# A graph network on one core: the stored one-hot matrix and the attention sums in f32, and a second score split into a linear word and a relu

## The reference

```
e = leaky_relu(x_l[src] + x_r[dst], 0.2) @ att
alpha = softmax of e over the edges of a destination (and a self loop)
out = segment_sum(alpha * x_l[src], dst) + bias
```

## Time and profile before

| what | value |
|---|---|
| median of three executions | 4830.54 us |
| profiled execution, its own time | 4824.61 us |
| span of the profile | 4822.8 us |
| message stage, first to last scatter | 303.6 to 1389.3 us |
| first attention, first gather to first row of the next stage | 1885.2 to 3003.7 us |
| second attention, first gather to first row of the next stage | 3107.5 to 4463.2 us |
| busy share of the span: PE, DVE, ACT, POOL | 49%, 58%, 13%, 56% |

### The profile page before, as it was taken

One profiled execution on the slowest core, in us unless ns is written; L12 is line 12 of the kernel. 1 busy time (PEld: TensorE's weight loads), 2 busy tenths in 40 slices (PEclk: granted clock), 3 DMA queues, 4 the chain that ended last, 5 costly groups with the idle time before them and its releaser, 6 DMA issues. The chain is left out here.

```text
span 4822.8 us, 75928 instructions
## 1 busy us (share of the span) xinstructions
PE 2356.4 (49%) x18851; PEld 1736.9 (36%) x18904; DVE 2781.6 (58%) x5419; ACT 647.4 (13%) x1473; POOL 2686.7 (56%) x2730
## 2 busy tenths in 40 slices
PE   0133333333306624666666665355555555555798
PEld 0023333333305513454544454233333333333232
DVE  8641111111118865777777777577877887877201
ACT  0001111111105410111111111011111111111000
POOL 0037777777745522777777774176666666663000
PEclk9955555555555555566666656555555555555899
DMA  0133334343315523555555552143333333332744
GB/s 21 38 123 124 125 122 130 126 129 123 114 36 109 107 47 85 140 144 148 143 147 147 143 146 78 42 102 94 94 95 91 91 97 92 94 95 60 275 170 168
DMA packets 533005, 537.07 MB, mean 111 GB/s; under 512 B 213790, under 2 KB 370324, under 8 KB 532618
## 3 DMA queue, kind: packets, MB, share of 16 engines
q1 hardware_dynamic: 243738, 289.79, 20.1%
q0 software_dynamic: 81072, 115.39, 10.7%
q10 hardware_dynamic: 208000, 130.01, 8.8%
HBM read 376.99 MB, written 159.58 MB: 111 GB/s over the span
## 5 line engine op out<-in xcount | busy, mean ns | idle before, releaser
L1381 POOL DMA_INDIRECT rows<-nodes_xl,id_slot x832 | 868.3, 1044 | 577.8 <-issue 240.9
L638 POOL DMA_INDIRECT msg_by_src<-message,place_slot x832 | 832.6, 1001 | 343.5 <-issue 252.8
L1381 POOL DMA_INDIRECT rows<-nodes_kv,id_slot x832 | 822.6, 989 | 339.8 <-issue 242.0
L1697 PE MATMUL counts_p<-hot_blocks 128*128 128x128 bf16 x2080 | 541.1, 413 | 362.3 <-DVE running_counts L1569 319.8
L599 PE MATMUL picked<-X,hotT 128*128 x1664 | 374.5, 423 | 674.2 <-issue 390.3
L599 PEld LDWEIGHTS picked<-X,hotT 128*128 128x128 f32 x1664 | 360.6, 331 | 688.0 <-issue 688.0
L560 DVE TENSOR_TENSOR message<-picked,w_dst 128x512 f32<-128x512 f32 x104 | 71.9, 691 | 845.7 <-ACT message L612 838.0
L1738 PE MATMUL sums<-parts,hot 128*128 128x68 bf16 (+1 forms) x4992 | 325.2, 251 | 374.9 <-DVE parts L1558 374.9
L1697 PEld LDWEIGHTS counts_p<-hot_blocks 128*128 128x128 bf16 x2080 | 277.5, 148 | 545.0 <-DVE running_counts L1569 339.1
L1738 PEld LDWEIGHTS sums<-parts,hot 128*128 128x128 bf16 x4992 | 311.8, 168 | 424.1 <-issue 424.1
L1569 DVE SCALAR_TENSOR_TENSOR running_counts<-running_counts,same_block,counts_p 128x128 f32<-128x128 f32 x1040 | 359.8, 346 | 171.0 <-DVE running_counts L1569 31.3
(11 more groups left out here) (343 smaller groups left out, 3606.2 us busy)
## 6 DMA issues: line engine op xcount, KB each, us to landing
adjacency<-running_counts ACTq DMA_DIRECT2D x1040, 64.0 KB
loc_all<-loc_by_cell SPq DMA_DIRECT2D x104, 512.0 KB
hotT<-hotT_by_step SPq DMA_DIRECT2D x208, 256.0 KB, 3.1
hot<-hot_by_step SPq DMA_DIRECT2D x208, 256.0 KB, 3.1
blocks<-adjacency SPq DMA_DIRECT2D x40, 1280.0 KB, 11.4
hot_by_step<-hot ACTq DMA_DIRECT2D x104, 256.0 KB, 2.0
hotT_by_step<-hotT ACTq DMA_DIRECT2D x104, 256.0 KB, 2.2
rows<-msg_by_src SPq DMA_DIRECT2D x312, 68.0 KB
```

Source lines behind the costliest of these rows:

```text
L638: pool.indirect_dma_start(out=msg_dram, out_offset=bass.IndirectOffsetOnAxis(ap=ids[:, s, t:t + 1], axis=0), in_=rows[:, s, t, :], in_offs ...
L1381: pool.indirect_dma_start(out=rows[:, j, t, :], out_offset=None, in_=table, in_offset=bass.IndirectOffsetOnAxis(ap=ids[:, j, t:t + 1], axis=0)
L1697: ins = nc.tensor.matmul(counts_p[:, q - HALVES[half][0], :], hot_b[:, r, 1, :, t], hot_b[:, r, 0, :, t], start=g == 0, stop=g == 1)
```

## The change

Four things are done.

- `hot` is f32 instead of bf16, in DRAM too (512 KB a step instead of 256). Line 567 reads the f32 lane number (repeated over the tiles) and the f32 places (repeated over the lanes), with the lane innermost, so that a tile's weights are contiguous. The two bf16 copies that it read go.
- The three parts, their two roundings on ScalarE and two subtractions on VectorE are gone. The sums are one f32 product for each tile, from `mixed` directly.
- `mixed` and `hot` have four slots, one for each step of a window. hot is loaded by SyncE in pairs in the steps s = 2 and 3, each behind a wait for the sums of the same slot one window before. `weigh` waits for the same sums.
- The second score is 0.2 y + 0.8 relu(y), y = x_l + x_r. The sum over words of 0.2 att x_l is one word per row, computed before the stage and stored as the 66th word of the table; the relu and the product with 0.8 att are one instruction; the word is added to the sum in a small one. The linear word of the destination is left out, for it is the same for all edges of a softmax.

The diff, cut to its core:

```
-        hot_dram = dram("hot_by_step", [STEPS, P, TB * P], BF16)
+        hot_dram = dram("hot_by_step", [STEPS, P, TB * P])
...
-                    step(v.tensor_copy(loc_h[:].rearrange("p j t -> p (j t)"), loc[:]))
...
-                    nc.vector.tensor_copy(lane_h[:], lane[:].unsqueeze(2).to_broadcast([P, P, TB])).then_inc(cleared, 1)
...
                         nc.vector.tensor_tensor(
-                            hot[:, s, :, :], lane_h[:],
-                            loc_h[:, bass.ds(i * NS + s, 1), :].rearrange("p a t -> p (a t)").unsqueeze(1).to_broadcast([P, P, TB]),
+                            hot[:, s, :, :], lane[:].unsqueeze(1).to_broadcast([P, TB, P]),
+                            loc[:, bass.ds((i * NS + s) * TB, TB)].unsqueeze(2).to_broadcast([P, TB, P]),
                             ALU.is_equal).then_inc(hot2_made[s], 1)
...
-                mixed = sbuf("mixed", [P, 2, TB, cols], ctx=c)
-                left = sbuf("left", [P, 2, TB, cols], ctx=c)
-                parts = sbuf("parts3", [P, 2, 3, TB, cols], BF16, ctx=c)
-                hot = sbuf("hot", [P, 8, P, TB], BF16, ctx=c)
+                mixed = sbuf("mixed", [P, 4, TB, cols], ctx=c)
+                hot = sbuf("hot", [P, 4, TB, P], ctx=c)
...
+                        def hot_loads(w, pair):
+
+                            for q in pair:
+                                if not (isinstance(w, int) and w == 0):
+                                    sp.wait_ge(scattered, w * 4 + q - 3)
+                                sp.dma_start(hot[:, q, :, :].rearrange("p t e -> p (t e)"),
+                                             hot_dram[bass.ds(w * 4 + q, 1), :, :].rearrange("a p e -> p (a e)")).then_inc(hot_in[q], 16)
...
-                            if w is not None and s >= 2:
-                                pair = (2 * s - 4, 2 * s - 3)
-                                for q in pair:
-                                    act.wait_ge(weighed, (w * 4 + q) * KM + KM)
-                                    if not (isinstance(w, int) and w == 0 and q < 2):
-                                        act.wait_ge(scattered, w * 4 + (q - 1))
-                                    nc.scalar.copy(parts[:, q % 2, 0, :, :], mixed[:, q % 2, :, :]).then_inc(high_made, 1)
-                                for q in pair:
-                                    act.wait_ge(left_made, w * 4 + q + 1)
-                                    nc.scalar.copy(parts[:, q % 2, 1, :, :], left[:, q % 2, :, :]).then_inc(middle_made, 1)
...
-                            if not (isinstance(w, int) and w == 0 and q < 2):
-                                dve.wait_ge(scattered, J - 1)
+                            if not (isinstance(w, int) and w == 0):
+                                dve.wait_ge(scattered, J - 3)
...
-                                    split(w, 0)
-                                    split(w, 1)
-                                    lowest_part(w, 0)
-                                    lowest_part(w, 1)
...
-                            pe.wait_ge(low_made, J + 1)
+                            pe.wait_ge(weighed, (J + 1) * KM)
                             for b, n in enumerate(ns):
                                 for t in (2 * b, 2 * b + 1):
-                                    for m in range(3):
-                                        ins = nc.tensor.matmul(sums[:, bass.ds(n, cols)], hot[:, p * 4 + q, :, t], parts[:, q % 2, m, t, :],
-                                                               start=False, stop=False)
+                                    ins = nc.tensor.matmul(sums[:, bass.ds(n, cols)], hot[:, q, t, :], mixed[:, q, t, :],
+                                                           start=False, stop=False)
...
-                    step(v.memset(xl[:, :, D:], 1.0))
+                    step(v.memset(xl[:, :, D:D + 1], 1.0))
+                    step(v.tensor_scalar(att_r[:], att_s[:], 0.8, None, ALU.mult))
+                    step(v.tensor_tensor(sq[:], lr[:, :, 0:D], rowwise(att_s[:]), ALU.mult))
+                    step(v.tensor_reduce(a[:], sq[:], AX.X, ALU.add))
+                    step(v.tensor_scalar(xl[:, :, D + 1], a[:], 0.2, None, ALU.mult))
...
-                step(v.scalar_tensor_tensor(leaky[:], product[:], 0.2, product[:], ALU.mult, ALU.max))
-                step(v.tensor_tensor(product[:], leaky[:], att_s[:].unsqueeze(1).to_broadcast([P, TB, D]), ALU.mult))
+                step(v.scalar_tensor_tensor(product[:], product[:], 0.0, att_r[:].unsqueeze(1).to_broadcast([P, TB, D]),
+                                            ALU.max, ALU.mult))
                 step(v.tensor_reduce(to, product[:], AX.X, ALU.add))
+                step(v.tensor_tensor(to, to, rows[:, :, D + 1], ALU.add))
```

More of the change, by code:

```diff
@@ L525, in messages @@
                 hotT_h = sbuf("hotT_16", [P, NS, TB, P], BF16, ctx=c)
-                hot = sbuf("hot", [P, NS, P, TB], BF16, ctx=c)
-                lane_h = sbuf("lane_h", [P, P, TB], BF16, ctx=c)
+                hot = sbuf("hot", [P, NS, TB, P], ctx=c)
                 picked = psum("picked", [P, NS, TB, D], c)
@@ L1351, in step @@
                                          hotT_dram[bass.ds(J, 1), :, :].rearrange("a p e -> p (a e)")).then_inc(hotT_in[j % 4], 16)
-                            if w is not None:
-                                hot_load(w, 1 - j // 4, j % 4)
+                            if w is not None and s >= 2:
+                                hot_loads(w, (2 * s - 4, 2 * s - 3))
                             if ef:
@@ L1546, in weigh @@
                             else:
-                                v.tensor_tensor(mixed[:, q % 2, :, 0:cols - 1], rows[:, slot, :, value_at:value_at + cols - 1],
+                                v.tensor_tensor(mixed[:, q, :, 0:cols - 1], rows[:, slot, :, value_at:value_at + cols - 1],
                                                 at.unsqueeze(2).to_broadcast([P, TB, cols - 1]), ALU.mult).then_inc(weighed, 1)
-                                v.tensor_copy(mixed[:, q % 2, :, cols - 1], PT[:, R + q * TB:R + (q + 1) * TB]).then_inc(weighed, 1)
-                        def split(w, q):
-                            dve.wait_ge(high_made, w * 4 + q + 1)
-                            v.tensor_tensor(left[:, q % 2, :, :], mixed[:, q % 2, :, :], parts[:, q % 2, 0, :, :], ALU.subtract
-                                            ).then_inc(left_made, 1)
-                        def lowest_part(w, q):
-                            dve.wait_ge(middle_made, w * 4 + q + 1)
-                            v.tensor_tensor(parts[:, q % 2, 2, :, :], left[:, q % 2, :, :], parts[:, q % 2, 1, :, :], ALU.subtract
-                                            ).then_inc(low_made, 1)
+                                v.tensor_copy(mixed[:, q, :, cols - 1], PT[:, R + q * TB:R + (q + 1) * TB]).then_inc(weighed, 1)
                         def chain(i, j, half):
@@ L1622, in step @@
                                 chain(i, j, 0)
-                            if w is not None and s == 3:
-                                split(w, 2)
-                                split(w, 3)
-                                lowest_part(w, 2)
-                                lowest_part(w, 3)
                         run(dve, step)
@@ L1895, in _ @@
                     sp.wait_ge(s, 16 * (len(pairs) + 1))
-        nodes_dram = {k: dram(f"nodes_{k}", [NPAD, w]) for k, w in (("kv", 2 * D + HEADS), ("xl", D + 1))}
+        nodes_dram = {k: dram(f"nodes_{k}", [NPAD, w]) for k, w in (("kv", 2 * D + HEADS), ("xl", D + 2))}
         X = sbuf("X", [P, NT, D])
```

52 lines of the change are left out of this document (23 added, 29 removed).

## The result

The change makes the kernel slower: 4872.87 us (median of four, 4871.63 to 4874.93) against 4830.07 for the kernel before in the same comparison, a ratio of 1.009 (95% interval 1.0072 to 1.0107). 4650 was forecast; the range ended at 4690. The profiled execution has a span of 4869.5 us, 47 more than before.

The account below looks back on a forecast made before the run. GpSimd's own pace was taken to bound the message stage and first attention, VectorE's chain the second attention. 4824.6 + 43 - 28 - 196 + 2 = 4646, predicted as 4650 us because runs' median lies 6 us higher; range 4604 to 4690.

Parts of the forecast that it names:

- The rival that held it: TensorE: f32 weight loads cannot run beside products, 3.6 us a step's sums, windows 51 us, about 4830; chance 0.02.
- The rival of a higher stop: Second attention: TensorE's sums, rows' arrival or GpSimd's hold-ups keep windows at 46 us, +50, 4700 us; chance 0.15.
- Messages, +43: Message stage: the longer two-input f32 comparison of line 567 holds up GpSimd's DMAs, 43 us longer.
- the upper bound: Message stage: about 60 us longer if the fourth step's DMA is hit too, starting inside the later line 578.
- the forecast's round: Message stage, four steps: hold-ups of 0.64 + 0.84 + 0.71 + 0 = 2.19 us against 0.54 before.
- The rival of no toll: Message stage: the longer f32 instruction holds GpSimd no longer, 4607 us; chance 0.17.
- First attention, -28: First attention: GpSimd's pace alone counts; -17 us from fewer hold-ups and -11 at the end.
- the sign that the forecast named: First attention: VectorE now idle before line 1980, with the rows' DMA as releaser.
- Second attention, -196: Second attention: windows fall from 51.6 to 43.9 us, VectorE's chain staying the bound; with the last stretch, -196 us.
- The subtractions' term: Second attention: eight VectorE subtractions a window go with the idle time before them, -5.9 us a window.
- The ends: Last stretches of the attentions: -11 us in the first, -12 in the second, from dropped subtractions and shorter waits.
- The slow rival: Halved ring of hot: loads land late, TensorE and GpSimd stop, 9 us a window lost in both attentions, 4880; chance 0.02.

Follow-up runs that it names:

- half of the sums: Kernel after with every second product of the sums left out, four a step instead of eight: 4692.64 us, 0.9716 of the kernel before.
- half of the columns: Kernel after with all f32 products kept, each on only the first half of its columns: ratio 1.0115 to the kernel before, on a slower chip.

## Why the prediction was wrong, point by point

**The step that failed** is one term: "an f32 product with f32 weights of 128x128 takes 7.09/32 = 0.222 us, a step's eight sums 1.78 us". The row is right and the division is not. It shows 32 instructions, and a product is two of them, so that a product takes 7.09/16 = 0.443 us and a step's eight 3.5 us. The row itself says it when its count is set against the code: line 599 has 8 products a step, and 32 MATMULs in one go are two steps' worth of picks only at two instructions each, since over the stage x1664 stand for 832 products. The forecast's own have this count too: x1657 in a stretch where TensorE has nothing but these 832 products. I read the count of the group as a count of products, because for bf16 it is one (x48 for two steps of 24). The bf16 parts took 3 x 0.065 = 0.196 us a product; the f32 product takes 2.3 times as long as all three, not 1.13 times.

**What followed from it.** In the second attention the second half of the products costs 5.4 us a window, 50.4 less 45.0, for which the forecast had nothing. TensorE has 2 x (7.09 - 3.5) = 7 us more a window, and part of it lies beside VectorE's other work. Of the 223 us between 4650 and 4873, 180 are this one (kernel after minus half of the sums); the other 42 would have missed the range by 3 us all the same.

**The rival that held it** was priced well and given 2 in 100. It named 3.6 us a step, counts late by 3.6 us, windows of 51 and 4830; measured are 3.5, a wait of 4.80, 50.4 and 4873. What it missed was the first attention, and the two ends. Its reason (f32 weight loads that set the pace) agrees with half of the columns, and the evidence against it, the row of 32 in 7.09 us, had the same wrong division in it. A rival whose only refutation is the number that the forecast rests on is not refuted. The rival of a higher stop, given 15 in 100, named the right stage and TensorE's sums as one of its reasons, but 2 us a window where 6.5 came.

**Messages, +43.** Right: +47, by the mechanism and the instruction named. Line 563 takes 1.21 us (1.23 forecast), the mean DMA 1057 ns (1050), and the stage ends at 1436 (1432). The four steps of a round hold up by 0.52, 0.61, 0.71 and 0.69 us in the stretch from 481 to 515 us, so all four are hit, as the upper bound had it, the first by line 574, which begins 0.1 us before its DMA; line 574 holds one more DMA of the round, by 0.31 us. Before, line 578 had also held more than the forecast's round allowed, so that the excess over 0.972 us a DMA rises from 23.9 to 70.6 us, by 47 and not by 60. The rival of no toll, and the inference of the Trainium skill (SBUF — State Buffer, Who interferes with whom) that a tensor_tensor leaves descriptor generation alone, fall: with both inputs in SBUF the DMA takes up to 1.68 us in that stretch, with one of them in PSUM 0.97. The section's other sentence, on two SBUF inputs, agrees.

**First attention, -28.** The subtractions and their hold-ups went (GpSimd's mean 989 to 976 ns), but GpSimd did not stay the bound. With TensorE busy for 822 of 1000 us the chain of VectorE and TensorE takes 42.5 us a window against 41.8 before; the forecast gave it 36 or less. The waits over 2200 to 2900:

```profile
DVE running_counts L1545 <- PE counts_p L1662: 62.9, 16, 3.9
DVE held L1455 <- PE turn_p L1670: 52.7, 16, 4.6
...
POOL rows L1377 <- DVE mixed L1528: 21.3, 17, 2.3
```

VectorE waits for counts, which it did not before, and more for the turned maxima behind the sums (34.2 us before in this stretch), and GpSimd, which should not have waited at all, waits for the weigh. With half of the sums the stage gives -19 of the 28, and there the sign that the forecast named appears: VectorE waits 118.5 us for gathered rows over the same stretch.

**Second attention, -196.** The forecast put TensorE's whole effect on a window at +0.3 us. The wait for the counts alone grew by 4.1 us a window, and the wait before the addition to the totals, which it had at nothing, is 1.5. The subtractions' term cannot be parted from TensorE's by these runs, the score's can: -2.1 forecast, -1.6 beside f32 sums and -2.4 beside bf16 ones. With half of the sums the stage gives -166, windows of 45.0 for 43.9.

**The ends.** I expected -11 and -12 us there. The final additions wait 9.6 to 9.7 us longer instead: at the end of a stage TensorE does 64 instructions in one go (13.9 us) with nothing of VectorE's beside them. With half of the products the waits are 5.5 and 5.4 us.

**hot in four slots and the doubled stores** cost nothing that shows. Before the sums of the kernel after TensorE is idle for 79.0 us in all, 69.3 of them for the weigh of the second attention and 9.6 for that of the first, so that nothing is left for a load of hot that comes late. The slow rival falls. Its price was also added up wrongly: 9 us in each of 26 windows are 234 us, and 4880 counts them for one attention, not for both. The preparation of the linear word costs the 2.5 us that were forecast: from the final addition of the first attention to the first gather of the second it is 112.4 us for 109.9.

## What to carry to other kernels

Before a duration is divided by the count of a row, set the count against the code's: an f32 product is two instructions, and the page's total for the line (x3328 for 1664 products) shows it at once. An engine with much idle time can still be the bound when its work comes in one piece ahead of something short that another engine waits for; here the same products, cut into pieces of one step and spread over the window, gave 127 us. When a hold-up is removed from one instruction, look at what moves into its place.

## What the runs showed of the hardware

An f32 product of 128x128 weights with 66 columns takes 0.443 us (7.09 us for 16), a bf16 one 0.065 (3.13 us for 48), both at a granted clock of 0.50 over the stretch of the row, the lower level of 1.2 GHz. That is 6.8 times as long, and with half of the columns it stays the same. The load rows beside them, 6.90 us for 32, are 0.216 us an instruction, two to a product. Part of the 0.443 is the end of the last product: 32 products take 13.92 us and 16 take 7.09, so each further one takes 0.427.

The Trainium skill (FP8 and Floating Point Precision, TensorE Precision Notes) gives a true f32 product four passes through the array; by passes alone, four times the bf16 product's 0.065, it would be 0.26 us by estimate, which the rows contradict. With a load for each pass, at the skill's columns divided by 1.2 GHz (TensorE: Matmul & The Clock Gate, LDWEIGHTS (loading the stationary operand)), it would be 4 x 128/1.2 = 0.427 us by estimate, and the measured 0.427 agrees. That there are four loads is not seen in the trace, which shows two. For bf16 the same figure gives 0.107 us a load by estimate, where a product with its own load follows every 0.065 us here, so that it does not hold for those.

The granted clock fell with the change: from 0.62 to 0.56 in the first attention and from 0.54 to 0.50 in the second, while TensorE's busy time rose from 647 and 642 to 822 us. It does not simply follow the busy time: with half of the sums TensorE is busy for 697 of the 1000 us of the first attention, and the clock there is 0.56 all the same, and 0.50 in the second. So the clock is not what half of the sums gave back. The counts of six take 1.55 to 1.60 us in both kernels, so little of the result can come from it; what it costs was not tried.

A hold-up of GpSimd's descriptor work goes with the inputs, not the operation: the 1024-wide f32 comparison of 1.21 us with one input in PSUM hardly lengthens a DMA that starts inside it (78 starts in the stage, in sum below 0.1 us), with both in SBUF it does (77 starts, 49.6 us). A tensor_scalar (line 578, 0.74 us) with one wide SBUF input and a column of scalars holds it too, to 1.25 us; the forecast named it only in its upper bound.
